# Queries and probability sums of the position products laid out with the image innermost

## The reference

```python
attn = jnp.einsum('bhqd,bhkd->bhqk', q, k) * scale
r_p_k = tab_kv[iv] + tab_kh[ih]           # (q, k, d): rows picked by vertical and horizontal distance
attn = attn + jnp.einsum('bhqd,qkd->bhqk', q, r_p_k) * scale
attn = jax.nn.softmax(attn, axis=-1)
out = jnp.einsum('bhqk,bhkd->bhqd', attn, v)
r_p_v = tab_vv[iv] + tab_vh[ih]
out = out + jnp.einsum('bhqk,qkd->bhqd', attn, r_p_v)
```

## Time and profile before

| what | value |
|---|---|
| median of 3 runs | 5201.05 us (5198.89 to 5211.17) |
| the profiled execution | 5215.72 us, span 5214.0 us |
| TensorE busy over the span | 4763.4 us (91%) |
| VectorE busy | 3365.6 us (65%) |
| ScalarE busy | 2270.1 us (44%) |
| GpSimd busy | 561.3 us (11%) |
| mean granted TensorE clock | 0.953 |

### The profile page before, as it was taken

One profiled execution on the slowest core, in us unless ns is written; L12 is line 12 of the kernel. 1 busy time (PEld: TensorE's weight loads), 2 busy tenths in 40 slices (PEclk: granted clock), 3 DMA queues, 4 the chain that ended last, 5 costly groups with the idle time before them and its releaser, 6 DMA issues. The chain is left out here.

```text
span 5214.0 us, 92414 instructions
## 1 busy us (share of the span) xinstructions
PE 4763.4 (91%) x31272; PEld 4490.0 (86%) x31272; DVE 3365.6 (65%) x9549; ACT 2270.1 (44%) x6372; POOL 561.3 (11%) x529
## 2 busy tenths in 40 slices
PE   4775799899899899989989999998999799999999
PEld 4765699899899889989988988998998699999999
DVE  4555566667666756766666676676666566666666
ACT  2443555555455545555555545555553122222221
POOL 1122000000000000000000000000000333333332
PEclk9887899999999999999999999999999899999999
DMA  6452000000000000000000000000000100000000
GB/s 138 99 123 62 6 1 1 1 20 1 1 20 1 1 2 20 1 1 20 1 1 20 1 1 1 20 1 1 10 1 3 42 16 18 18 18 16 16 18 18
DMA packets 65157, 99.50 MB, mean 19 GB/s; under 512 B 3763, under 2 KB 60674, under 8 KB 61120
## 3 DMA queue, kind: packets, MB, share of 16 engines
q1 hardware_dynamic: 61312, 90.31, 6.9%
q0 software_dynamic: 944, 2.42, 0.3%
q10 hardware_dynamic: 2560, 2.36, 0.2%
HBM read 65.88 MB, written 29.20 MB: 18 GB/s over the span
## 5 line engine op out<-in xcount | busy, mean ns | idle before, releaser
L643 ACT ACTIVATE att_prob<-att_s,att_npeak 99x198 f32<-99x198 f32 x1536 | 638.8, 422 | 1229.6 <-DVE att_npeak L816 1186.5
L816 DVE TENSOR_REDUCE att_npeak<-att_s 99x2 f32<-99x396 f32 x768 | 436.2, 568 | 901.1 <-PE att_s L988 899.0
L971 PE MATMUL att_o<-att_probT,att_vx 99*96 99x198 f32 (+1 forms) x3072 | 686.1, 346 | 1.3 <-ACT att_probT L633 1.3
L988 PE MATMUL att_s<-att_kx,att_qx 96*99 96x198 f32 (+1 forms) x3072 | 659.2, 337 | 3.6 <-DVE att_xres L782 2.7
L1351 PE MATMUL ffn_y<-ffn_down,ffn_hidden 128*128 128x192 f32 x3564 | 637.4, 329 | 6.8 <-DVE ffn_acc L1262 4.9
L1351 PEld LDWEIGHTS ffn_y<-ffn_down,ffn_hidden 128*128 128x128 f32 x3564 | 590.0, 191 | 29.4 <-DVE ffn_acc L1262 27.5
L971 PEld LDWEIGHTS att_o<-att_probT,att_vx 99*96 99x96 f32 (+1 forms) x3072 | 511.6, 182 | 42.3 <-issue 32.7
L988 PEld LDWEIGHTS att_s<-att_kx,att_qx 96*99 96x99 f32 (+1 forms) x3072 | 518.6, 169 | 19.0 <-issue 4.6
L806 DVE TENSOR_SCALAR att_prob<-att_prob,att_total 99x198 f32<-99x198 f32 x1536 | 459.1, 342 | 26.9
L1132 POOL TENSOR_TENSOR ffn_hidden<-ffn_relu 128x384 f32<-128x384 f32 x462 | 378.7, 826 | 764.9 <-ACT ffn_relu L1159 457.2
L1159 ACT ACTIVATE ffn_relu<-ffn_h 128x384 f32<-128x384 f32 x231 | 113.0, 489 | 705.7 <-PE ffn_h L1340 705.5
(11 more groups left out here) (208 smaller groups left out, 9611.7 us busy)
## 6 DMA issues: line engine op xcount, KB each, us to landing
tok_pixels<-in_x SPq DMA_DIRECT2D x24, 1568.0 KB
ffn_hid<-hidden SPq DMA_DIRECT2D x34, 288.0 KB, 2.9
att_xres<-hidden SPq DMA_DIRECT2D x8, 1188.0 KB
hidden<-att_xres SPq DMA_DIRECT2D x8, 1188.0 KB
out_hidden<-ffn_acc SPq DMA_DIRECT2D x33, 288.0 KB, 2.3
hidden<-tok_rows SPq DMA_DIRECT2D x8, 1176.0 KB
att_oT<-in_L_attn_qkv_w ACTq DMA_DIRECT2D x1, 1536.0 KB, 11.1
tok_posb<-in_L_tok_pos_embedding POOLq DMA_DIRECT2D x1, 1176.0 KB, 42.4
```

The source lines that it names most:

```text
L643: ins = nc.scalar.activation(prob[:, i % 2, h, :], s_bank[i % 2][0:HALF, h * NTOK:(h + 1) * NTOK], ACT.Exp, bias=npeak[:, i % 2, h:h + 1], ...
L816: nc.vector.tensor_reduce(npeak[:, i % 2, :], s_bank[i % 2][0:HALF, 0:2 * NTOK].rearrange("p (h k) -> p h k", h=2), AX.X, ALU.max, negate= ...
L971: ins = nc.tensor.matmul(o_bank[j % 2][0:M, 0:NTOK], vx[:, p % 2, 2 * b + k, v0:v0 + M], probT[:, j % 2, k * NTOK:(k + 1) * NTOK], start=( ...
L988: ins = nc.tensor.matmul(s_bank[i % 2][0:HALF, h * NTOK:(h + 1) * NTOK], qx[0:K, p % 2, head, q0:q0 + HALF], kx[0:K, p % 2, head, b * NTOK ...
```

## The change

`q2` and `rx` keep their size, but number (b, n) now stands at n x 8 + b: the eight images of a token are neighbours. Nothing moves between steps or engines, no instruction is added or taken away, and all other tiles keep their layout. What changes is the access of the instructions around the two tiles:

- TensorE reads a row of the grid as 112 neighbouring numbers, and a column as 14 runs of 8 neighbouring numbers (32 bytes), 448 bytes from run to run. Its result in PSUM is in the same order, image innermost, and is written as one run.
- ScalarE's copy into `q2` (line 611) writes single numbers 32 bytes apart, in two blocks of 198. VectorE's copy into `rx` (line 796) writes 198 single numbers 32 bytes apart.
- What reads the results out of PSUM (ScalarE line 621, VectorE lines 755, 763, 772) reads them with the image as outer dimension. For row passes the inner step becomes 8 numbers (32 bytes), where it was 1. For column passes the inner step becomes 112 numbers, where it was 14. What they write, or add onto, in `qx` and `oT` is as before.

```diff
         def group_rhs(src, a):
             off, n, step = q_cols(a)
-            return view(src, [[NTOK, GB], [step, n]], off)
+            return view(src, [[step * GB, n], [1, GB]], off * GB)
+
+        def by_image(src, n):
+            return view(src, [[1, GB], [GB, n]])
+
+        def by_image_cols(src, n):
+            return view(src, [[1, GB], [GB, SIDE], [SIDE * GB, n]])
...
-                        nc.scalar.activation(q2[:, cols], bank[:, 0:HC], ACT.Copy, scale=SCALE)
+                        nc.scalar.activation(view(q2[:, :], [[1, HC // NTOK], [GB, NTOK]], j * HC // NTOK),
+                                             bank[:, 0:HC].rearrange("p (b n) -> p b n", n=NTOK), ACT.Copy, scale=SCALE)
...
                             ins = nc.scalar.activation(view(qx[lo:lo + 32, s, head, :], [[NTOK, GB], [1, n]], first),
-                                                       view(bank[src:src + 32, :], [[n, GB], [1, n]]), ACT.Copy)
+                                                       by_image(bank[src:src + 32, :], n), ACT.Copy)
...
                             ins = nc.vector.tensor_tensor(
-                                dst, view(bank[src:src + 32, :], [[n * SIDE, GB], [1, SIDE], [SIDE, n]]), dst, ALU.add)
+                                dst, by_image_cols(bank[src:src + 32, :], n), dst, ALU.add)
...
-                        ins = nc.vector.tensor_tensor(dst, view(bank[:, :], [[n, GB], [1, n]]), dst, ALU.add)
+                        ins = nc.vector.tensor_tensor(dst, by_image(bank[:, :], n), dst, ALU.add)
...
-                    nc.vector.tensor_copy(rx[ext:ext + 32, p % 2, cols], o_bank[j % 2][ext:ext + 32, 0:NTOK]
+                    nc.vector.tensor_copy(view(rx[ext:ext + 32, p % 2, :], [[GB, NTOK]], b), o_bank[j % 2][ext:ext + 32, 0:NTOK]
                                           ).then_inc(outs_used, 1)
...
                         for a, col in ROWBANKS[j - 8]:
-                            ins = nc.tensor.matmul(view(bank[0:64, :], [[n, GB], [1, q_cols(a)[1]]], col), tq[:, a, :],
+                            ins = nc.tensor.matmul(bank[0:64, col * GB:(col + q_cols(a)[1]) * GB], tq[:, a, :],
                                                    group_rhs(q2[:, :], a), start=True, stop=True)
...
-                            ins = nc.tensor.matmul(view(bank[0:64, :], [[n * SIDE, GB], [1, SIDE]], i * SIDE), tq[:, 16 + 13 - c, :],
+                            ins = nc.tensor.matmul(bank[0:64, i * SIDE * GB:(i + 1) * SIDE * GB], tq[:, 16 + 13 - c, :],
                                                    group_rhs(q2[:, :], 16 + 13 - c), start=True, stop=True)
```

More of the change, by code:

```diff
@@ L772, in job @@
                         ins = nc.vector.tensor_tensor(
-                            dst, view(bank[:, :], [[n * SIDE, GB], [1, SIDE], [SIDE, n]]), dst, ALU.add)
+                            dst, by_image_cols(bank[:, :], n), dst, ALU.add)
                     elif kind == "last":
@@ L912, in job @@
                     elif kind == "first" and j < 12:
-                        n = ROWSPAN[j - 8][1]
                         for a, col in ROWBANKS[j - 8]:
-                            ins = nc.tensor.matmul(view(bank[0:64, :], [[n, GB], [1, q_cols(a)[1]]], col), tq[:, a, :],
+                            ins = nc.tensor.matmul(bank[0:64, col * GB:(col + q_cols(a)[1]) * GB], tq[:, a, :],
                                                    group_rhs(q2[:, :], a), start=True, stop=True)
@@ L931, in job @@
                     elif j < 4:
-                        n = ROWSPAN[j][1]
                         for a, col in ROWBANKS[j]:
-                            ins = nc.tensor.matmul(view(bank[:, :], [[n, GB], [1, q_cols(a)[1]]], col), tv[:, a, :],
+                            ins = nc.tensor.matmul(bank[:, col * GB:(col + q_cols(a)[1]) * GB], tv[:, a, :],
                                                    group_rhs(rx[:, s, :], a), start=True, stop=True)
@@ L939, in job @@
                         for i, c in enumerate(span):
-                            ins = nc.tensor.matmul(view(bank[:, :], [[n * SIDE, GB], [1, SIDE]], i * SIDE), tv[:, 16 + 13 - c, :],
+                            ins = nc.tensor.matmul(bank[:, i * SIDE * GB:(i + 1) * SIDE * GB], tv[:, 16 + 13 - c, :],
                                                    group_rhs(rx[:, s, :], 16 + 13 - c), start=True, stop=True)
```

## The result

The changed kernel is 1.1% slower: 5261.57 us median of 4 runs (5250.12 to 5268.44) against 5202.67 (5198.89 to 5211.17), also of 4 runs, before: a ratio of 1.0109 with a 95% interval of 1.0086 to 1.0131. The profiled execution took 5264.03 us, 48 more than that of before, with a mean granted clock of 0.935 where it was 0.953.

The account below looks back on a forecast made before the run. TensorE was taken to bound the kernel, with column passes 236 us cheaper, of which VectorE leaves 180; stepped PSUM reads and SBUF writes cost nothing. 5201 - 180 = 5021 us, range 4962 to 5130.

Parts of the forecast that it names:

- What bounds the kernel, and what a column product costs: Attention stage: TensorE sets the pace; column products drop from 0.195 and 0.193 to 0.103 and 0.110 us, 236 us altogether.
- Reading PSUM with a step: VectorE's additions and ScalarE's line 621 read PSUM in new steps: claimed to cost nothing.
- Writing SBUF with a step ... I take nothing: Lone-number writes of lines 796 and 611: claimed to cost nothing, bounded by 1.74 ns a number.
- Rival 1: Lone writes are paid at 1.74 ns: ScalarE 68 us, VectorE 38 us, so 5127 us; chance 0.28.
- What VectorE leaves of it: Steps 7 to 10: VectorE's chains and additions leave 3.74 us a unit of TensorE's 4.90, 180 us over 48 units.
- Rival 2: ScalarE pays for lone numbers in PSUM too, line 621: 135 us on top of Rival 1, 5262 us; chance 0.07.
- Rival 3: Banks never hold TensorE up, also in the last units: all 236 us come off, 4965 us; chance 0.10.
- what the profile after would show: Expected signs: column starts 0.10 and 0.11 us apart, copy times unchanged, TensorE idle about a microsecond a unit in steps 7 to 10.

Follow-up runs that it names:

- j: Changed kernel, but both copies write contiguously (products read wrong numbers) and column jobs alternate with value jobs in units 0 to 4: 5005.6 us, 0.9621 of before.
- a: Changed kernel, but both copies write contiguously as before the change, so products read numbers of the wrong image and token: 5128.2 us, 0.9859 of before.
- l: Kernel before with only the two copies changed to write lone numbers, TensorE reading as before (wrong numbers): 5330.9 us, 1.0247 of before.
- i: Changed kernel with four extra products in TensorE's wait in step 8 of units 0 to 4: 5184.1 us, 0.9952 of before.
- m: Kernel before with two more TensorE waits for VectorE's additions in step 8 of 30 units: 5303.3 us, 1.0189 of before.
- n: Kernel with only q2 changed, plus one extra product in TensorE's wait in step 8: 5234.4 us, 1.0051 of before.
- c: Changed kernel with only rx in the new layout, q2 written and read as before: 5173.9 us, 0.9946 of before.
- h: Changed kernel, but VectorE adds only one head for two column jobs of step 7, leaving additions out: 5178.9 us, 0.9956 of before.

## Why the prediction was wrong

**What bounds the kernel, and what a column product costs: right.** Starts on line 927 are 0.099 us apart (0.103 forecast), 0.096 on most of them; on line 945 0.112 on most (0.110). Two busy times of the attention stage were read off slightly wrong, 2274 and 1785 us for the 2270 and 1792 of the row, and nothing hangs on them. Experiment j turns 197 of the 236 us into time, so they were there to be had.

**"Reading PSUM with a step": right.** 631 for 629 ns on VectorE, 541 for 540 on ScalarE.

**"Writing SBUF with a step ... I take nothing": wrong, and the larger of the two failed steps.** VectorE's copy pays (522 - 359) / 198 = 0.82 ns a number on top of 1.07, ScalarE's (906 - 502) / 396 = 1.02 on top of 0.85: 1.9 ns for a lone number on both, a little over the 1.74 that I bounded it with. I had let a copy of 15 numbers decide against the additions of two-number runs, which pointed the right way. Here the rule of the Trainium skill, page "SBUF — State Buffer", section "Specifications (TRN2)", that full rate needs at least two accesses to a line of 16 bytes, held for writes as for reads: two numbers to a line brought the copy from 906 back to 546 ns. Rival 1 had this mechanism and priced it at 106 us; a and l measured 133 and 128. Its split was another: ScalarE's part is 1.0 us a unit, in steps 0 and 2, and not 1.41, while the last unit of a group, which it counted as the others, pays 5.4 us, and the granted clock falls more often.

**"What VectorE leaves of it": the place and the wait right, the sum wrong.** The wait was forecast at 4.90 - 3.74 = 1.16 us a unit; it is 66.7 us in all with free writes and 73.7 as changed, 1.4 to 1.5 us a unit. What the step left out is the granted clock behind the wait: it took a microsecond of waiting to cost a microsecond. With free writes (a) the clock was low for 126 us in steps 8 and 9 against 27 before, 50 us of time; as changed for 160, and i gained 78 by keeping it up. Had the writes been free, the forecast would have been 107 us off: some 50 are the clock, about 11 the longer wait, about 9 the last units of the groups, which I had counted like the others and which gave 2.6 us each instead of 3.74, and about 7 a step 12 that is 0.17 us longer; the rest I can't place singly.

**The rivals.** Rival 2 named 5262 and the time is 5261.6, by accident: its mechanism, ScalarE paying for steps in PSUM, isn't there. The 241 us between forecast and result are 133 of lone writes and 107 that are there without them, most of it wait and clock. Rival 3 (all of the gain, 4965) is what j, at 5006, comes nearest to once the order of jobs is another. In the list of what the profile after would show, "TensorE should now be idle for about a microsecond in a unit" held (1.6 to 1.9 us, all in step 8), and the consequence of it was not drawn.

## What to carry to other kernels

A layout that makes one reader fast makes the writers slow, so count each writer's lone numbers at the reader's own price unless a row as long as the real one says otherwise, and look for a way to write two at a time. When the bounding engine is sped up in a few steps, sum up the next engine's work in those steps; if it comes near, interleave them with work that does not load it (139 us here, and nothing in the kernel before). Where the clock's rows show it falling behind waits, price an idle microsecond of TensorE at about two (48 us of waits cost 98 in m, and useless work in waits of 75 us was worth 78 in i). Where they don't show it, as in step 0 here, leave the clock out.

## What the runs showed of the hardware that was not expected

- In step 8 of the changed kernel waits of 1.7 to 2.0 us on TensorE, once a unit, are followed by 3.4 to 6.8 us of granted clock at half in 38 of 39 units; filled with products they are not (i, 0 for 160 us). Two waits of 0.8 us in the kernel before did the same (m, 188 for 27 us).
- Waits of 1.05 to 1.95 us in step 0 of the same 39 units are followed by next to none (6 us of low clock in all), and with free writes (a) waits of 1.5 to 1.8 us in step 8 are followed by low clock in 21 of 39 units only.
- The clock also falls with little or no idle time (126 us in n with 0.25 us a unit, 75 us in l with none), and doesn't with waits of 0.8 us in c and h (0 us).
- The instruction behind a copy of lone numbers pays as well: line 619 took 547 ns for 485, on ScalarE, though its own access is unchanged.
- Lone numbers cost 1.9 ns when written by ScalarE or VectorE, against 1.74 when read by TensorE; in PSUM, steps of 32 to 792 bytes cost the readers nearly nothing (VectorE 2 ns in 448 numbers, ScalarE at most 44 ns in 396).
